# Expert weighing moved to the head of each block, and the first block's sliding maxima turned later

## The reference, cut to what matters

```python
xn = _layernorm(x)
x = x + L0_attn(xn) + L0_ffn(xn)     # L0_attn: out = concat(lin, win) @ Wout; x + out
xn = _layernorm(x)
x = x + L1_attn(xn) + L1_ffn(xn)

def _L1_ffn_ref(x, Wg, W1, b1, W2, b2):
    logits = xt @ Wg.T
    topk_logits, topk_idx = jax.lax.top_k(logits, TOP_K)     # 2 of 8
    w = jax.nn.softmax(topk_logits, axis=-1)
    gates = jnp.zeros((T, N_EXPERTS)).at[rows, topk_idx].add(w)
    h = gelu(jnp.einsum('th,ehi->tei', xt, W1) + b1)
    o = jnp.einsum('tei,eih->teh', h, W2) + b2
    y = jnp.einsum('te,teh->th', gates, o)
```

## Time and profile before

| | us |
|---|---|
| median of 3 runs (1351.23, 1357.06, 1356.45) | 1356.45 |
| the profiled execution | 1351.23 |
| its span, first to last instruction | 1349.2 |
| PE busy, share of the span | 1235.1, 92% |
| DVE busy | 812.3, 60% |
| ACT busy | 713.4, 53% |
| POOL busy | 602.2, 45% |

### The profile page before, as it was taken

The page is one execution under the profiler, slowest core; times in us unless marked ns, Lnnn a source line. Parts: engine busy times, 40 slices in busy tenths (PEclk is TensorE's granted clock), DMA queues, the critical chain, the costliest instruction groups (busy, mean ns, idle before and its releaser), DMA issues. The chain is left out here.

```text
span 1349.2 us, 26273 instructions
## 1 busy us (share of the span) xinstructions
PE 1235.1 (92%) x9090; PEld 868.6 (64%) x9090; DVE 812.3 (60%) x3359; ACT 713.4 (53%) x1532; POOL 602.2 (45%) x793
## 2 busy tenths in 40 slices
PE   4998999999999999999999999999999837689997
PEld 2465576657765776577657765776577625389997
DVE  4065387638853886388538853885388448356663
ACT  2266267625772577257725772576257602457675
POOL 6133153515441544154425442544254533658787
PEclk9999999999999999999999999999999977889999
DMA  9403430243023302340234023402340034034443
GB/s 268 112 3 89 109 80 9 88 107 90 9 87 93 105 9 87 86 112 9 87 87 110 10 88 86 110 11 82 91 108 13 10 87 160 29 58 67 58 68 45
DMA packets 82227, 101.83 MB, mean 75 GB/s; under 512 B 12472, under 2 KB 43104, under 8 KB 82016
## 3 DMA queue, kind: packets, MB, share of 16 engines
q1 hardware_dynamic: 60160, 80.24, 22.1%
q0 software_dynamic: 14304, 10.61, 5.0%
q10 hardware_dynamic: 7632, 9.31, 2.2%
HBM read 55.44 MB, written 46.37 MB: 75 GB/s over the span
## 5 line engine op out<-in xcount | busy, mean ns | idle before, releaser
L955 ACT ACTIVATE probs<-bank 128x512 f32<-128x512 f32 (+2 forms) x896 | 441.7, 582 | 259.7 <-PE bank L578 254.6
L578 PE MATMUL bank<-K,Q 128*128 128x192 f32 (+4 forms) x1024 | 243.1, 317 | 15.0 <-issue 13.6
L1132 POOL TENSOR_SCALAR_AFFINE_SELECT probs<-probs 128x384 f32<-128x384 f32 x256 | 127.0, 518 | 282.5 <-ACT probs L955 281.4
L578 PE MATMUL bank<-Q,K 128*128 128x192 f32 (+4 forms) x1024 | 216.4, 318 | 2.9 <-DMA Q<-mrow_c 2.6
L635 PE MATMUL heads<-probs,V 128*9 128x192 f32 (+4 forms) x3072 | 196.1, 396 | 14.2 <-DVE probs L1375 5.6
L578 PEld LDWEIGHTS bank<-K,Q 128*128 128x128 f32 x1024 | 170.2, 193 | 42.6 <-issue 27.5
L578 PEld LDWEIGHTS bank<-Q,K 128*128 128x128 f32 x1024 | 150.9, 192 | 33.3 <-issue 19.0
L635 PEld LDWEIGHTS heads<-probs,V 128*9 128x9 f32 x3072 | 75.6, 91 | 125.8 <-issue 82.9
L945 ACT ACTIVATE probs<-bank,sh_s 128x512 f32<-128x512 f32 x64 | 44.0, 687 | 212.5 <-PE bank L571 201.8
L578 PE MATMUL bank<-QM,K 128*128 128x512 f32 (+3 forms) x512 | 137.6, 332 | 11.2 <-DVE mx_s L1323 6.3
L1186 POOL DMA_INDIRECT out<-h1T_s x78 | 122.8, 1574 | 46.6 <-issue 26.9
(11 more groups left out here) (190 smaller groups left out, 2061.9 us busy)
## 6 DMA issues: line engine op xcount, KB each, us to landing
Q<-slots_of_q SPq DMA_DIRECT2D x16, 1024.0 KB, 10.5
K<-slots_of_k SPq DMA_DIRECT2D x64, 192.0 KB
QM<-slots_of_qm SPq DMA_DIRECT2D x8, 1024.0 KB, 9.0
slots_of_q<-Q SPq DMA_DIRECT2D x24, 256.0 KB, 3.0
slots_of_k<-QM SPq DMA_DIRECT2D x24, 256.0 KB, 4.0
slots_of_qm<-Q SPq DMA_DIRECT2D x24, 256.0 KB, 4.2
slots_of_k<-Q SPq DMA_DIRECT2D x24, 256.0 KB, 3.0
slots_of_q<-Q ACTq DMA_DIRECT2D x24, 256.0 KB, 4.8
```

The source lines that it names most:

```text
L578: mm = pe.matmul(to[:, at:at + right.shape[1]], left, right, start=True, stop=True, skip_group_check=True)
L955: return act.activation(to, bank, func, scale=scale, bias=bias).then_inc(taken_sem(run, unit), 1)
L1132: pool.affine_select(out=three, in_=three, compare_op=ALU.is_ge, fill=0.0, base=0, pattern=[[0, 3], [1, P]], channel_multiplier=-1)
```

## The change

It does two things.

1. weigh_experts of the block before moves from after the third layer's sum (d = 8) to the head of pairs_stage, ahead of every maximum, and in the tail ahead of place_rows. The wait for rows_filled goes from place_rows to weigh_experts, ahead of its last instruction, and place_rows waits for gates_filled. The instructions are the same ones.
2. turned_at() is gone; the sliding maxima are turned at n = 31 in all parts. For part "first", where it was 0, this moves turn_max on PE, negate_max and first_stats on DVE, and the unit slide_max in the rotation of the banks; in the other parts nothing moves.

```diff
-def turned_at(before):
-    return 31 if before else 0
@@ pairs_order
-            (["slide_max"] if n == turned_at(before) else [])
+            (["slide_max"] if n == 31 else [])
@@ PE, beside_causal
-                    if n == turned_at(before):
+                    if n == 31:
                         turn_max(run, "slide_max", mx_s[:, :], SMAX_UNITS[-1])
@@ DVE
             def weigh_experts(now):
                 dve.wait_ge(S["exped"], due("exped", now, 1))
                 ...
-                lap("choice_laps", now, 13, dve.tensor_tensor(wide, flat, gates...
+                lap("choice_laps", now, 9, dve.tensor_tensor(wide, flat, gates...
+
+                dve.wait_ge(S["rows_filled"], due("rows_filled", now, 2))
                 dve.tensor_reduce(rows[:, :, :, P], wide, AX_X, ALU.add).then_inc(S["gates_filled"], 1)
             def place_rows(run, now):
+                dve.wait_ge(S["gates_filled"], due("gates_filled", now, 1))
                 dve.wait_ge(full_sem(run, "prefix"), full_at(run, "prefix"))
                 ...
-                dve.wait_ge(S["rows_filled"], due("rows_filled", now, 2))
@@ DVE, pairs_stage
+                if before:
+                    weigh_experts(previous)
                 ...
-                    if a == PAIRS + turned_at(before):
+                    if a == PAIRS + 31:
                         negate_max(run, "slide_max", mrow_s)
                         if after:
                             first_stats((b, 1))
                 ...
                             .then_inc(taken_sem(run, "third_layer"), 1)
-                        if before:
-                            weigh_experts(previous)
```

More of the change, by code:

```diff
@@ L1396, in choose_experts @@
                 dve.wait_ge(S["picked"], due("picked", now, 1))
[L1398 to L1404, removed]
-                dve.wait_ge(S["rows_filled"], due("rows_filled", now, 2))
-                lap("choice_laps", now, 8, dve.tensor_reduce(slot[:, :].rearrange("p (t k) -> p t k", k=K2), wide, AX_X, ALU.add))
-                lap("choice_laps", now, 9, dve.tensor_copy(slot_i[:, :], slot[:, :]))
-                dve.sem_inc(S["placed"], 1)
             def weigh_experts(now):
@@ L1413, in weigh_experts @@
                 dve.wait_ge(S["exped"], due("exped", now, 1))
-                lap("choice_laps", now, 10, dve.scalar_tensor_tensor(out=exs[:, :, :], in0=rank[:, :, :], scalar=1.5, in1=ex[:, :, :], op0=ALU.is_lt, op1=ALU.mult))
-                lap("choice_laps", now, 11, dve.tensor_reduce(gsum[:, :], exs[:, :, :], AX_X, ALU.add))
-                lap("choice_laps", now, 12, dve.reciprocal(rsum[:, :], gsum[:, :]))
+                lap("choice_laps", now, 6, dve.scalar_tensor_tensor(out=exs[:, :, :], in0=rank[:, :, :], scalar=1.5, in1=ex[:, :, :], op0=ALU.is_lt, op1=ALU.mult))
@@ L1420, in weigh_experts, with place_rows @@
+                dve.wait_ge(S["rows_filled"], due("rows_filled", now, 2))
                 dve.tensor_reduce(rows[:, :, :, P], wide, AX_X, ALU.add).then_inc(S["gates_filled"], 1)
+            def place_rows(run, now):
+                wide = by_expert(place[:, :, :])
+                dve.wait_ge(S["gates_filled"], due("gates_filled", now, 1))
+                dve.wait_ge(full_sem(run, "prefix"), full_at(run, "prefix"))
+                prefix = bank_of(run, "prefix")[:, 0:(NT + 1) * K2 * E].rearrange("p (t n) -> p t n", t=NT + 1)
+                lap("choice_laps", now, 10, dve.tensor_tensor(place[:, :, :], prefix[:, 0:NT, :], base[:, :].unsqueeze(1).to_broadcast([P, NT, K2 * E]), ALU.add))
+                dve.tensor_tensor(base[:, :], prefix[:, NT, :], base[:, :], ALU.add).then_inc(taken_sem(run, "prefix"), 1)
+                lap("choice_laps", now, 11, dve.tensor_tensor(place[:, :, :], place[:, :, :], picks[:, 0:NT, :], ALU.mult))
+                lap("choice_laps", now, 12, dve.tensor_reduce(slot[:, :].rearrange("p (t k) -> p t k", k=K2), wide, AX_X, ALU.add))
+                lap("choice_laps", now, 13, dve.tensor_copy(slot_i[:, :], slot[:, :]))
+                dve.sem_inc(S["placed"], 1)
```

4 lines of the change are left out of this document (3 added, 1 removed).

## The result

The kernel after the change takes 1395.27 us (median of 5 runs, 1393.34 to 1397.72), the kernel before 1357.06 (5 runs, 1351.23 to 1360.23): a ratio of 1.0284, 95% interval 1.027 to 1.0298. It is slower, by 38 us between the medians. The prediction was 1380, with a range up to 1392: the direction was right, the size too small, and the time lies outside the range.

What follows compares the result with a forecast made beforehand. PE was taken as the bound, busy 1235.1 of 1349.2 us. Heads 18.6, fetch -2.2, clock 5.9 and block 0 4.2 sum to 26.5 us: 1377.7 on the profiled execution, 1383 on the median, forecast 1380, range 1368 to 1392.

Steps and rivals of the forecast that it cites:

- the six instructions at the head: Heads of blocks 1 to 7: weigh_experts takes 1.28 us on DVE, its wait for rows_filled adding at most 0.1.
- the clock: Seven heads: PE's clock falls behind the pause with chance 0.6, costing 1.4 us each time; 5.9 in all, bounds 0 and 11.9.
- the clock's term: Block 0: clock lost in PE's pause of 4.7 us adds 1.0 us.
- DVE's wait at the head: Heads of blocks 1 to 7: DVE stands from 170.0 to 173.3 for exped; SMAX 0 starts 3.81 us late.
- PE's pause behind its seventh unit: Each head: PE uses up its seven banks and pauses 3.1 to 3.2 us until the bank of SMAX 0 is free.
- the pause of 1.01 that goes: Behind the third layer's sum in blocks 1 to 7: PE's 1.01 us pause vanishes, leaving each block 2.65 late.
- the fetch that absorbs a little: First causal maximum, blocks 3 to 6: PE arrives later and finds the queries landed, saving 2.2 us in all.
- Rival C: Heads: banks and the later pause mostly absorb the delay, about 1 us a block left; 10 in all, 1361 to 1366; chance 0.07.
- D: Heads: the 1.01 us pause goes and the wait is covered, so faster by 4 us, 1347 to 1352; chance 0.02.
- E: Heads: exped is there in time in later blocks; about +3 us from block 0 alone, 1354 to 1360; chance 0.03.
- Rival B: Clock falls at every head, 7 x 1.7 = 11.9 us, and block 0 costs 5; 33 in all, 1384 to 1390; chance 0.12.
- The first term: Block 0: turning the maxima later delays the sliding scores, which go on at 111.0 instead of 107.81; 3.2 us.

Runs made afterwards that it cites:

- filler: The kernel after, plus 16 matmuls whose result nothing reads in PE's pause at the heads of blocks 1 to 7: 1378.8 us, ratio 1.0176.
- rows_first_filler: The kernel after, with POOL's copies into rows ahead of its power and 14 unread matmuls in PE's pause at each head: 1378.3 us, ratio 1.0152.
- wait_filler: The kernel before, with only a DVE wait for exped at the head, plus 8 unread matmuls in PE's pause there: 1375.33 us, ratio 1.014.
- turn_moved_only: The kernel before with only block 0's sliding maxima turned at n = 31, weigh_experts where it was: 1359.56 us, ratio 1.0031.
- weigh_at_places: The kernel before, with weigh_experts moved right ahead of place_rows at d = 5, block 0's maxima unmoved: 1353.09 us, ratio 0.9968.
- weigh_before_sum_14: The kernel before, with weigh_experts ahead of the wait for the third layer and 14 instead of 12 sliding maxima before the first causal one: 1350.51 us, ratio 0.9952.
- wait_only: The kernel before, with only a DVE wait for exped added at the head and no instruction moved: 1380.24 us, ratio 1.018.
- scores_first: The kernel after, with the first five LIN units ahead of SMAX 0 at each head of blocks 1 to 7: 1385.97 us, ratio 1.0221.
- turn_moved_filler: The kernel before with block 0's maxima turned at n = 31, plus 20 unread matmuls in block 0's pause: 1358.92 us, ratio 1.0027.

## Why the prediction was right or wrong

Two terms of the sum failed: the six instructions at the head were given the 1.28 us that they take elsewhere, without a collision (none forecast, 0.72 per head measured), and the clock was given 0.6 times 1.4 us per head (5.9 in all), where it fell at every head and cost 1.90 (13.3 in all). In block 0 the clock's term was too small as well.

**Right: where, and the stall.** DVE's wait at the head (3.34 by the trace), PE's pause behind its seventh unit and released by the maxima, the pause of 1.01 that goes (none is left in filler and rows_first_filler), and the fetch that absorbs a little. The forecast was 2.65 - 2.2/7 = 2.34 per head; rows_first_filler, where this alone is left, has 2.40, and wait_filler 2.48. Rival C (mostly absorbed), D and E are out: the period grew by 5.

**Missed: the collision.** The step "the six took 1.28 us from the first's start to SMAX 8's start" took its duration from a place where POOL stood idle: before the change nothing of POOL runs from 176.2 to 180.0. At the head DVE is released by the end of POOL's power, and POOL's next instruction is the copy: the release itself makes them meet. The view of line 1396 of the kernel after shows it at all eight places ( count, min, median and max ns, first and last start):

```profile
L1396 DVE SCALAR_TENSOR_TENSOR exs<-rank,ex x8: 920/926/928, 179.6 to 1150.2; 128x32 f32<-128x32 f32 x8
```

It costs 0.72 per head, 5.0 us in all. The Trainium skill, "SBUF — State Buffer", section "Who interferes with whom", says that a DVE instruction with two inputs in SBUF contends with a GpSimd instruction that reads SBUF, since its second input comes through the read interface that the two share, and that the shared ports are an exclusive lock. The trace agrees: exs (rank and ex, both in SBUF) ends 0.04 us behind the copy, and is back at 0.19 when the copy is elsewhere.

**Mis-sized: the clock.** "A chance of 0.6 at each of the seven heads and 1.4 us each time" gave 5.9. It fell at seven of seven and cost 1.90: 13.3, above the forecast's upper bound of 11.9. Rival B had "falls at every head"; its price of 1.7 is what one low stretch of 3.4 us in the tail loses at half speed, and here six of seven stretches were twice as long. Against filler's 139.4 the three distances with 6.8 us that began near the pause's end or behind it cost 2.2 to 2.6, the two in which they began earlier in the pause 1.4 and 1.7, and the one with 3.4 us 1.1. The evidence for a chance as low as 0.6 was the opening's pause of 2.12 at full clock, and it was one draw: with the same code the clock fell behind that pause in three of 14 traces. What makes it fall in seven of seven behind 1.9 us at the heads and in three of 14 behind 2.12 in the opening is not shown. The heads differ in that PE is released bank by bank afterwards, while in the opening eight matmuls follow in one piece, but no run isolated that. The rule of the Trainium skill that the prediction weighed ("TensorE: Matmul & The Clock Gate", section "A second HAM failure mode: psum-queue depth-cycling") spoke for a fall at every head; the trace agrees there, and disagrees before the change, where pauses of 1.0 in the same rotation kept 1.00.

**Block 0.** Forecast 3.2 + 1.0, measured 6.38 in the kernel after and 6.10 in turn_moved_only. The first term is right (3.35 with the pause filled); the clock's is 2.75, not 1.0. Behind the pause of 4.65 PE does the first sliding scores and the turn of hrow at a granted clock of 0.50 (the ten matmuls in 2.45 instead of 1.36), and a second low stretch of 3.4 us follows from about 130. Both stretches are in all six traces that have this pause unfilled. Part of it can still be chance: in weigh_at_places and weigh_before_sum_14, where block 0 is the code of before and PE's pauses there are under 1 us, the clock fell at 108 and block 0 took 98.69 and 98.68.

**Not foreseen, and not shown to belong to the change: the end.** The last distance lost 1.98 more than a head, and the tail 1.76. Windows over the end of block 7 and the start of the tail in the kernel after:

```profile
1084.00:1120.00 36.00, 31.82 (x357) 23.46 (x360) 19.10 (x60) 23.04 (x54) 19.02 (x31) 1.00 0.04 10
1120.00:1160.00 40.00, 19.29 (x101) 13.96 (x93) 18.72 (x62) 2.15 (x3) 14.75 (x12) 0.59 0.46 133
```

This is the sparse stretch that the kernel before has too, at 0.70 in its 1084 to 1110. In wait_only, which moves no instruction, the last distance also lost more than a head, by 1.1 (120.72 - 115.90 - 3.70); in filler it lost less, 2.17 where a head lost 3.12. What follows the last power took 247.9 us before and 249.7 in turn_moved_only, whose code there is that of before. Differences of 2 us at the end are thus as large as those between traces of equal code, and the 3.6 us can't be put down to a cause.

| term, us | forecast | profile |
|---|---|---|
| seven heads: stall less fetch | 16.4 | 7 x 2.40 = 16.8 |
| seven heads: collision with the copy | none | 7 x 0.72 = 5.0 |
| seven heads: clock | 5.9 | 7 x 1.90 = 13.3 |
| block 0: pause | 3.2 | 3.35 |
| block 0: clock | 1.0 | 6.38 - 3.35 = 3.0 |
| end of block 7 and tail, start | 0 | 1.98 + 1.76 - 0.16 = 3.6 |
| sum | 26.5 | 45.1 |

Of the 18.6 us missed, 9.4 are the clock, 5.0 the collision and 3.6 the end. Between the medians it is 38.2, not 45.1, since the profiled execution of the kernel before was the fastest of its five. It was also at a higher clock than others: 0.979, where the later repeats of that kernel beside the experiments have 0.963 to 0.976. This suggests, and no trace of a slower execution of that kernel shows it, that its usual execution loses a few microseconds to falls of the clock that are not in the trace the sum was worked out from.

What stays open: why the clock falls behind one pause and not behind another of the same length, why the low stretch lasts 3.4 us at some heads and 6.8 at others, and the 3.6 us at the end.

## What to carry to other kernels

Moving a wait to an engine that the busiest one follows can cost more than the stall: add what the pause does to PE's clock. One trace in which the clock held behind a similar pause is a weak reason to halve that price; look at the same pause in several traces first, and at how long the low stretches last. When an instruction is released by another engine, look at what that engine does next, and whether both use the same port. And when a pause is removed, look for the next transfer that PE will meet early: of 1.01 us taken away here, 0.30 arrived per head, and 0.44 once the first use of the fetch stood later as well.

## What the runs showed of the hardware

- Behind pauses of 1.9 us the granted clock went to 0.50 at seven of seven heads (wait_only, and scores_first too); behind the opening's 2.12 it did so in three of 14 traces. Pauses of 1.0 at the same heads before left it at 1.00, but not in every trace: in turn_moved_only the clock fell at the heads of blocks 2 and 4, behind pauses of 1.25 and 1.00, and in turn_moved_filler at those of blocks 1 and 7, behind 1.01 and 1.00. The heads' code is that of before in both. In turn_moved_only these falls are most of the 2.9 us that its heads cost. The windows:

```profile
320.00:328.00 8.00, 6.75 (x30) 5.68 (x30) 7.63 (x42) 5.47 (x10) 3.62 (x6) 0.79 0.09 32
594.00:602.00 8.00, 6.37 (x30) 5.55 (x31) 6.92 (x37) 4.94 (x10) 3.76 (x6) 0.79 0.06 18
```

- Sixteen extra matmuls at each head made the changed kernel faster: 1.0176 against 1.0284 of the time before.
- A DVE instruction of 0.18 us took 0.93 beside a copy of 1.03 on POOL, and 0.33 where only the copy's last 0.28 lay beside it (weigh_at_places).
- POOL's power of 128 x 32 took 5.55 us in every kernel, or 5.50 where the copies stood ahead of it.
